# GpSimd applies gain and shift of the first LayerNorm of the fused stage, and the statistics of the new tokens stand half a step later

## What is computed

```python
x = _layernorm(x + _moe(x, ...), ln3_g, ln3_b)      # end of layer 0, with gain and shift
...
residual = query                                    # layer 1: query is that x
qn = _layer_norm(query, ln1_g, ln1_b)
Q = (qn @ wq + bq); K = (kn @ wk + bk); V = (vn @ wv + bv)
attn = softmax(Q K^T / sqrt(HD)); out = attn V
x = residual + out @ wo + bo
y = gelu(_layer_norm(x, ln2_g, ln2_b) @ w1 + b1) @ w2 + b2
return x + y
```

## Time and profile before

| | |
|---|---|
| median of three runs | 1475.5 us (1467.96 to 1479.77) |
| span of the profiled execution | 1416.2 us |
| VectorE, ScalarE, GpSimd busy in it | 962.8, 993.5, 866.3 us |
| TensorE busy in it | 1253.1 us |

### The profile page before, as it was taken

The page is one execution under the profiler, slowest core; times in us unless marked ns, Lnnn a source line. Parts: engine busy times, 40 slices in busy tenths (PEclk is TensorE's granted clock), DMA queues, the critical chain, the costliest instruction groups (busy, mean ns, idle before and its releaser), DMA issues. The chain is left out here.

```text
span 1416.2 us, 59902 instructions
## 1 busy us (share of the span) xinstructions
PE 1253.1 (88%) x23136; PEld 1052.9 (74%) x23136; DVE 962.8 (68%) x2123; ACT 993.5 (70%) x2030; POOL 866.3 (61%) x1340
## 2 busy tenths in 40 slices
PE   4999999989999998668899999961699999998997
PEld 2778877777888887657899999960577777785775
DVE  3777777767787875588455555534799999963331
ACT  1777777767888885298566666641789999974553
POOL 1567667666766774310899999848677777423331
PEclk9999999999999998559899999985799999999999
DMA  3233323323232242052222222222233333121221
GB/s 108 70 94 93 111 90 96 99 85 91 82 89 81 81 129 76 8 183 70 61 67 69 68 67 70 65 62 65 76 90 92 92 94 91 52 61 53 71 70 45
DMA packets 140281, 113.91 MB, mean 80 GB/s; under 512 B 17184, under 2 KB 113952, under 8 KB 140192
## 3 DMA queue, kind: packets, MB, share of 16 engines
q1 hardware_dynamic: 131744, 95.42, 22.9%
q0 software_dynamic: 8448, 17.32, 4.9%
HBM read 78.55 MB, written 34.08 MB: 80 GB/s over the span
## 5 line engine op out<-in xcount | busy, mean ns | idle before, releaser
L832 DVE TENSOR_REDUCE at_mx<-at_ps_s 128x16 f32<-128x1024 f32 x128 | 156.1, 1220 | 106.8 <-PE at_ps_s L561 60.7
L761 ACT ACTIVATE at_pt<-at_ps_t 128x1024 f32<-128x1024 f32 x128 | 130.6, 1020 | 56.3 <-PE at_ps_t L575 55.4
L2225 POOL DMA_INDIRECT ex_xg<-x,ex_ti x136 | 148.0, 1088 | 23.3 <-issue 21.9
L754 ACT ACTIVATE at_pr<-at_dd 128x1024 f32<-128x1024 f32 x128 | 135.2, 1056 | 34.7 <-DVE at_dd L840 34.6
L2306 DVE COPY ex_wt<-experts 128x1156 f32 x136 | 104.8, 772 | 75.7 <-DVE ex_y L2312 72.9
L2285 ACT ACTIVATE ex_hg<-ex_ps_h,ex_wt 128x128 f32<-128x128 f32 x544 | 154.4, 372 | 1.3 <-PE ex_ps_y L2254 1.2
L840 DVE TENSOR_TENSOR at_dd<-at_ps_s,at_mx 128x1024 f32<-128x1024 f32 x128 | 153.7, 1202 | 0.1
L1860 POOL DMA_INDIRECT l_yg<-rows,l_sl x128 | 128.9, 1007 | 33.8 <-issue 30.5
L2245 PE MATMUL ex_ps_h<-ex_xt,ex_wt 128*128 128x128 f32 x1088 | 147.2, 279 | 0.0
L575 PE MATMUL at_ps_t<-ident,at_pr 128*128 128x128 f32 x1024 | 139.9, 280 | 5.2 <-issue 4.2
L2254 PE MATMUL ex_ps_y<-ex_wt,ex_hg 128*128 128x128 f32 x1088 | 143.7, 275 | 0.7 <-ACT ex_hg L2285 0.7
(11 more groups left out here) (240 smaller groups left out, 3174.9 us busy)
## 6 DMA issues: line engine op xcount, KB each, us to landing
rows<-ex_y SPq DMA_DIRECT2D x136, 64.0 KB
x<-at_ln_out SPq DMA_DIRECT2D x32, 256.0 KB, 3.2
at_kx<-in_xt SPq DMA_DIRECT2D x16, 256.0 KB, 2.8
at_qx<-in_xt SPq DMA_DIRECT2D x16, 256.0 KB, 2.8
at_vin<-in_xt SPq DMA_DIRECT2D x16, 256.0 KB, 2.7
at_xr<-in_x SPq DMA_DIRECT2D x16, 256.0 KB, 2.9
x1t<-at_xt SPq DMA_DIRECT2D x16, 256.0 KB, 3.3
at_kx<-in_ctxt SPq DMA_DIRECT2D x16, 256.0 KB, 2.8
```

The costliest lines, as they stand in the source:

```text
L754: act.activation(pr[:, p], dd[:, p], ACT.Exp, scale=SCALE).then_inc(p_ready, 1)
L761: act.activation(pt[:, 2 * h + p], ps_t[:, :, :, :], ACT.Copy).then_inc(pt_ready, 1)
L832: dve.tensor_reduce(mx[:, p], ps_s[:, :, 4 * p:4 * p + 4, :], AX.X, ALU.max).then_inc(mx_ready, 1)
L2225: pool.indirect_dma_start(out=xg[:, s, :], out_offset=None, in_=x_src, in_offset=bass.IndirectOffsetOnAxis(ap=ti[:, s:s + 1], axis=0)).the ...
```

## The change

The multiplication by the gain and the addition of the shift move from VectorE's program to GpSimd's. On VectorE they stood in step g for group g + 3; on GpSimd they stand in step g for group g + 2, the gain behind the second `spread`, the shift between gathers 3 and 4. The statistics of the new tokens move from the end of VectorE's step g - 1 to the middle of its step g, between `normalise` and `front_moments`. What each operation computes, and on which buffers, stays.

```diff
@@ VectorE
-                def gain_own(a):
-                    dve.wait_ge(z3_ready, a.g + 1)
-                    dve.tensor_tensor(zg3[:, a.u], z3[:, a.u], c.row["ln3_g"][:, None, :].broadcast_to([P, GP, D]),
-                                      ALU.mult).then_inc(zg3_ready, 1)
-
-                def shift_own(a):
-
-                    dve.wait_ge(zg3_ready, a.g + 1)
-                    dve.tensor_tensor(held(a), zg3[:, a.u], c.row["ln3_b"][:, None, :].broadcast_to([P, GP, D]),
-                                      ALU.add).then_inc(x3_ready, 1)
-
...
                     if a.shift(-1).exists():
                         normalise(a.shift(-1), 1)
+                    if a.shift(2).exists():
+                        next_statistics(a.shift(2))
                     if a.shift(3).exists() or a.shift(2).exists():
                         front_moments(a.shift(3))
...
                     if a.exists():
                         recip(g * 2, 0)
-                    if a.shift(3).exists():
-                        gain_own(a.shift(3))
                     if a.shift(-1).exists():
                         residual(a.shift(-1))
-                    if a.shift(3).exists():
-                        shift_own(a.shift(3))
                     if a.shift(1).exists():
                         maximum(g * 2 + 3, 0)
-                    if a.shift(3).exists():
-                        next_statistics(a.shift(3))
                     if a.exists():
                         normalise(a, 0)
@@ GpSimd
+                def gain_own(a):
+                    pool.wait_ge(z3_ready, a.g + 1)
+                    pool.tensor_tensor(zg3[:, a.u], z3[:, a.u], c.row["ln3_g"][:, None, :].broadcast_to([P, GP, D]),
+                                      ALU.mult).then_inc(zg3_ready, 1)
+
+                def shift_own(a):
+
+                    pool.wait_ge(zg3_ready, a.g + 1)
+                    pool.tensor_tensor(held(a), zg3[:, a.u], c.row["ln3_b"][:, None, :].broadcast_to([P, GP, D]),
+                                      ALU.add).then_inc(x3_ready, 1)
...
                     if a.shift(-1).exists():
                         spread(g * 2 - 1, 1)
+                    if a.shift(2).exists():
+                        gain_own(a.shift(2))
                     if a.shift(4).exists():
                         fetch(a.shift(4), 3, 4)
+                    if a.shift(2).exists():
+                        shift_own(a.shift(2))
+                    if a.shift(4).exists():
                         fetch(a.shift(4), 4, 5)
```

## The result

The changed kernel takes 1469.14 us (median of 20 executions, 1464.38 to 1471.88), the kernel before 1473.08 us in the same comparison (20 executions, 1466.02 to 1480.58). The ratio is 0.9965, with a 95% interval of 0.9952 to 0.9978: some 4 us faster, clear of the noise but less than the 1% (15 us) that the prediction set as the bound of what counts as a change. The forecast was 1500 us.

The account below looks back on a forecast made before the run. VectorE, with no idle left, set the pace; after the change POOL and the dependence on its shift would. 18 + 5.3 + 1.6 = +25 us on the 1416.2 us span gave 1441; set on the median, 1500 us, range 1486 to 1511.

Parts of the forecast that it names:

- start: Fused stage before its steady steps: +3.2 us up to the first scores and +2.1 in the first full step, together +5.3.
- first maximum: In the start, on DVE behind POOL's first four operations: gain, shift and statistics make it about 3 us later (+3.2).
- ten steady steps: Steady part of the fused stage, 1031.4 to 1205.0 us: +1.8 us a step, +18 us in all.
- end: Last steps of the fused stage: +1.3 us in the step from 1205 and +0.3 in the last, together +1.6.
- step: One steady step of the fused stage, from the start of POOL's four operations: 19.15 us against 17.36.
- the wait for the moments: POOL after gather 4, before its four operations: 0.7 us of each step is a new wait for DVE's moments.
- port rival: DVE's second weighing is held up until POOL's gain ends: steps of 19.6 us, +32 in all, 1507 us; chance 0.13.
- The 59.3 us: Median of the three runs, 1475.5 us, over the profiled span, 1416.2; taken as unchanged by the edit.

Follow-up runs that it names:

- lower level: Sessions in which the kernel before, unchanged, takes about 1419 us; the profiled execution behind the prediction, span 1416.2 us, is of this kind.
- upper level: Sessions in which the kernel before, unchanged, takes 1473 to 1488 us; the three runs beside the profile and the compared executions are of this kind.

## Why the prediction was wrong

**The sum was right, where its trace came from.** Forecast +25 us on a span of 1416.2; in a session of that level the spans differ by 28.0 us (1442.5 less 1414.5) and the times by 26. Term by term, from the begin of POOL's four operations in both traces:

| term | forecast | measured at the lower level |
|---|---|---|
| start (to the step at 1029.81 before, 1036.11 after) | +5.3 | +6.3, of which 0.9 lies ahead of POOL's first four operations (964.06, 964.99); first maximum 997.79 against 994.15, +3.6 (forecast +3.2) |
| ten steady steps | +18 | +19.0 (192.6 against 173.6) |
| end | +1.6 | +2.7, the rest of 28.0 |
| step | 19.15 us | 19.28 us |

The gain and the shift on POOL cost 1.32 and 1.28 (forecast 1.27 each), the wait for the moments 0.90 (0.7), and DVE was free for the statistics with the shift's end (17.26, statistics at 17.42). The times within the step are within 0.15 us of the forecast. (In the forecast's start the terms from the second reciprocal add up to 6.9, which is 2.0 over 4.87 and not 2.1; it changes nothing.)

**The port.** The second weighing on DVE takes 2.41 us there, with spread and gain beside it, against 1.46 with the spread alone in the same session. It ends at 1108.71, right behind the gain (1107.25 to 1108.57). That is the port rival's mechanism, and it did cost 0.95 us; but it cost the step little, since DVE then was free just as the shift ended. The Trainium skill, page "SBUF — State Buffer", section "Who interferes with whom", says that the second of the two to come is blocked; an end 0.14 us behind the gain's agrees with that.

**The step that failed** is the one that set the sum on the median: "what makes them up isn't in the profile, and I take it as unchanged". The 59.3 us were not something outside the span. The executions that were timed are not like the profiled one; a trace of this level shows what they do: steps of 21.65 us in place of 17.36, with pauses of TensorE. A term worked out in one trace was set on the time of another. The profile before had no row that shows it, but the section on the time before had the two numbers: a span 3.5% under the fastest of the three runs, where in all 19 later traces of this study span and time of the same execution differ by 1.7 to 2.5 us. That gap was the sign that the profiled execution was not of the same kind as the timed ones, and the range should have held a case for it.

**Where the 26 us went.** At the upper level the change costs the same chain, and gains somewhere else. This is read from traces of both levels. Before, the second burst of a step begins 1.2 us behind POOL's four operations (1101.38 against 1100.22), and gathers 5 to 7, which follow these, begin 1.4 us into it: four pauses, 5.1 us. In the changed kernel the handover and POOL's added work make POOL's four operations later against TensorE: the burst begins first (1100.06, POOL at 1101.05), and gathers 5 to 7 come at 1103.60, when it is over. It takes 2.06 us without a pause. The first burst keeps its pauses in both. Per step, the change adds 1.9 us of chain (lower level, 17.36 to 19.26 in the mean of ten), and the upper level adds 4.3 us before (21.65 less 17.36) but only 2.0 after (21.24 less 19.26). The bursts account for it to within 0.4 us: what they take over 1.99 us is 4.4 us a step before and 2.3 after, in the mean of ten steps. The saving of 2.3 outweighs the cost of 1.9 by some 0.4 a step: 4.1 us in ten steps. The start, 1.2 us later, and the last steps, some 0.9 shorter, about cancel, and the medians differ by 4 us. The delay of POOL's four operations, which the forecast had right and counted as pure loss, is itself what moves the gathers away. The run with the statistics alone has that gain without POOL's extra work (its gathers 5 to 7 begin 2.26 us behind the start of a second burst of 1.99 us), and gains 17 to 21 us; the kernels without gathers have neither gain nor pauses, and the change costs 19.5 us. That the saving came out about as large as the cost is a coincidence of two sizes.

What is shown and what isn't: that without gathers there are no pauses, that they go with the gathers from burst to burst, and that with them gone the change has the forecast sign, is shown by runs. That a plain transfer would not do the same rests on one burst. How a gather holds up TensorE's instructions, and what makes a session one of the upper level, is open. Blocks of instructions that are fetched from memory don't answer it. The part of the traces on DMA queues (queue and kind: packets, MB, share of 16 engines) has, from 1075 to 1300 us, this for the changed kernel, and this for the kernel before with TensorE's program written out:

```profile
q14 instruction: 5, 0.04, 0.1%
```

```profile
q8 instruction: 35, 0.57, 1.1%
q14 instruction: 4, 0.03, 0.0%
```

With the loop, five small blocks in 225 us; written out, 35 blocks of 16 KB more. Both have the pauses.

Whether the version with the statistics alone, the fastest with all its work at the upper level, also wins at the lower level wasn't measured; the estimate of its expectation is steps of 17.9 us against 17.36.

## What to carry to other kernels

Before a forecast worked out in a trace is added to a measured time, see that the profiled execution and the timed runs are of the same kind: a gap of more than a few us between them is a case of its own, to be priced. Where an engine's instruction is a gather, its time in the step matters beyond its own queue: ask beside which burst of another engine it falls before and after an edit, also when the edit moves it only by a wait. And a new wait isn't always a loss, as it shifts two engines against each other.

## What the runs showed of the hardware

- Beside gathers that GpSimd issues, TensorE pauses in a dense burst of small products (128 products of 64 columns and their weight loads in 1.99 us): 0.40 us at a time, 0.73 us apart, one to six in a row, in some sessions and not in others (0 pauses in 48 such bursts of three traces, 118 of 125 bursts in ten others). The first pause begins 0.81 us or more behind the start of a gather. The earlier attention layers, with the same bursts and no gathers beside them, have none in either.
- The Trainium skill, page "SBUF — State Buffer", section "Who interferes with whom", says of the engines' ports to SBUF that TensorE and ScalarE never wait on anyone. No row here names the port as the cause, but at the upper level GpSimd's gathers do hold TensorE up in some way: the same burst takes 1.99 us without them and, in the median, 4.26 to 4.65 us with them.
- A plain transfer of a 128x128 tile holds GpSimd for about 0.56 us (three in 1.70), an indirect one for 0.94 to 1.03 with 0.30 to the next.
- In the traces whose stretched bursts took 5.1 to 6.5 us, the granted clock of the stretch from 1037 to 1210 us fell to 0.92 to 0.98, to 0.50 right behind such a burst, and the products there ran longer (the output projection 2.03 to 2.08 us in place of 1.15). In the changed kernel and with the statistics alone, where they took 4.3 and 4.7 us, it stayed at 1.00.
